# Which copy of the scores the exponential of a split-precision attention reads, and when the residual input is loaded

## The reference

```python
q_hk = (hidden_q @ Wq.T).reshape(Bv, Sv, H, K)
q_big = _apply_rope(jnp.einsum('bshk,hkq->bshq', q_hk, w_kc_q), sin_q, cos_q)
kv_r = _apply_rope(kv_c, sin_k[None], cos_k[None])
q_r = jnp.einsum('bshq,hqr->bhsr', q_big, W_qr)
k_r = jnp.einsum('bld,hdr->bhlr', kv_r, W_kr)
attn = jax.nn.softmax(jnp.einsum('bhsr,bhlr->bhsl', q_r, k_r), axis=-1)
ctx_c = jnp.einsum('bhsl,bld->bhsd', attn, kv_r)
ctx_lat = jnp.einsum('bhsd,hkd->bhsk', ctx_c, w_kc_kv)
return ctx_lat.transpose(0, 2, 1, 3).reshape(Bv, Sv, H * K) @ Wo.T

x = x + _L0_xattn_ref(_layernorm(x), ctx_512, ...)
x = x + _L0_attn_ref(_layernorm(x), ...)     # heads mix inside one token, no softmax
x = x + _L0_ffn_ref(_layernorm(x), ...)      # silu(gate) * up, integer weights with scales
```

## Time and profile before

| | |
|---|---|
| median of 3 runs | 1104.91 us (1104.62 to 1105.61) |
| the profiled execution | 1106.48 us, span 1104.7 us |
| PE busy | 1033.1 us, 94% of the span |
| DVE busy | 855.7 us, 77% |
| ACT busy | 799.8 us, 72% |
| POOL busy | 498.4 us, 45% |
| 256 maxima, lines 973 | 217.0 + 109.8 us |
| 256 exponentials, line 673 | 204.4 + 103.4 us |
| 256 low halves, line 962 | 322.3 us, DVE idle before them 87.8 us |
| 256 split passes, line 664 | 270.6 us, ACT idle before them 34.0 us |
| transposing DMAs | 256, 3.8 us from issue to landing in the median |

### The profile page before, as it was taken

The page is one execution under the profiler, slowest core; times in us unless marked ns, Lnnn a source line. Parts: engine busy times, 40 slices in busy tenths (PEclk is TensorE's granted clock), DMA queues, the critical chain, the costliest instruction groups (busy, mean ns, idle before and its releaser), DMA issues.

```text
span 1104.7 us, 24584 instructions
## 1 busy us (share of the span) xinstructions
PE 1033.1 (94%) x9456; PEld 718.9 (65%) x9456; DVE 855.7 (77%) x1177; ACT 799.8 (72%) x1380; POOL 498.4 (45%) x748
## 2 busy tenths in 40 slices
PE   4899998999999999999799999999999899999988
PEld 3444444666666677667577766776777654859877
DVE  3999888989898988888698898888898813454633
ACT  1233338899999999999799998999999932426532
POOL 1985363566767554545345454545455312000000
PEclk9999999999999999999899999999999999999989
DMA  8443365899999999999999899999998952032000
GB/s 342 132 146 114 109 138 111 180 193 204 198 202 207 207 193 199 190 188 195 192 196 193 201 179 195 192 197 194 201 193 192 192 190 105 1 132 89 1 20 20
DMA packets 568917, 180.15 MB, mean 163 GB/s; under 512 B 551520, under 2 KB 557664, under 8 KB 568160
## 3 DMA queue, kind: packets, MB, share of 16 engines
q1 hardware_dynamic: 567184, 173.33, 72.3%
q10 hardware_dynamic: 1616, 5.24, 1.5%
HBM read 39.07 MB, written 1.05 MB: 36 GB/s over the span
## 4 chain that ended last, share of the span: by engine, by line
PE 57%; DMA 13%; DVE 13%; ACT 10%; issue 6%; POOL 0%; SPq 0%; ACTq 0%; POOLq 0%; DVEq 0%
DMA pt_both<-p_both 13%; PE ps_o L1289 6%; PE ps_o L1290 6%; PE ps_o L1293 5%; PE ps_o L1350 5%; ACT prob L673 5%; DVE sized L973 4%; PE ps_s L1270 3%; PE ps_s L1271 3%; PE ps_s L1272 3%; DVE qcos L892 2%; DVE qrot L888 2%; ACT p_both L664 2%; PE ps_t L1270 2%; ACT oscl L690 2%
## 5 line engine op out<-in xcount | busy, mean ns | idle before, releaser
L962 DVE SCALAR_TENSOR_TENSOR p_both<-prob,p_both 128x1024 f16<-128x1024 f32 x256 | 322.3, 1259 | 87.8 <-ACT p_both L664 87.2
L664 ACT ACTIVATE p_both<-prob 128x1024 f16<-128x1024 f32 x256 | 270.6, 1057 | 34.0 <-DMA pt_both<-p_both 11.7
L1289 PE MATMUL ps_o<-kn,pt_both 128*128 128x128 f16 x2048 | 257.1, 219 | 27.9 <-DMA pt_both<-p_both 27.4
L1290 PE MATMUL ps_o<-kn,pt_both 128*128 128x128 f16 x2048 | 257.0, 219 | 0.0
L1289 PEld LDWEIGHTS ps_o<-kn,pt_both 128*128 128x128 f16 x2048 | 200.0, 98 | 71.7 <-DMA pt_both<-p_both 27.0
L973 DVE TENSOR_SCALAR_CACHE_REDUCE sized<-ps_s,against 128x1024 bf16<-128x1024 f32 x170 | 217.0, 1276 | 0.0
L1290 PEld LDWEIGHTS ps_o<-kn,pt_both 128*128 128x128 f16 x2048 | 200.7, 98 | 24.7
L673 ACT ACTIVATE prob<-ps_s,nmax,unscale 128x1024 f32<-128x1024 f32 x170 | 204.4, 1202 | 11.9 <-DVE sized L973 11.8
L538 POOL TENSOR_TENSOR osum<-oscl 128x256 f32<-128x256 f32 x64 | 47.9, 749 | 257.9 <-ACT oscl L690 257.9
L1293 PE MATMUL ps_o<-kn,pt_both 128*128 128x128 f16 x2048 | 156.6, 219 | 0.0
L1270 PE MATMUL ps_s<-kt,q_hi 128*128 128x512 f16 x340 | 129.3, 380 | 3.5 <-ACT prob L673 2.6
(11 more groups left out here) (215 smaller groups left out, 1849.8 us busy)
## 6 DMA issues: line engine op xcount, KB each, us to landing
wgu_raw<-w_gu_dram SPq DMA_DIRECT2D x11, 512.0 KB, 10.0
wq_s<-wq_t_dram SPq DMA_DIRECT2D x16, 256.0 KB, 3.8
wot_s<-wo_t_dram SPq DMA_DIRECT2D x16, 256.0 KB, 2.8
kvr<-ctx_kv_dram ACTq DMA_DIRECT2D x4, 1024.0 KB, 12.4
pt_both<-p_both SPq DMA_TRANSPOSE x256, 3.8
kvr<-w_mix_dram SPq DMA_DIRECT2D x4, 1024.0 KB, 9.2
wkcq_s<-w_kcq_dram SPq DMA_DIRECT2D x16, 192.0 KB, 2.4
wdn_raw<-w_dn_dram SPq DMA_DIRECT2D x1, 2816.0 KB, 8.9
```

The source lines that it names most:

```text
L664: nc.scalar.mul(p_hi(n), prob[:, n % 2, :], PSCALE).then_inc(hi_done, 1)
L962: nc.vector.scalar_tensor_tensor(out=p_lo(n), in0=prob[:, n % 2, :], scalar=PSCALE, in1=p_hi(n), op0=ALU.mult, op1=ALU.subtract).then_inc( ...
L1289: nc.tensor.matmul(o, pt_hi[:, k, :], kn[:, b, p, 0, keys], start=(k == 0), stop=False)
L1290: nc.tensor.matmul(o, pt_hi[:, k, :], kn[:, b, p, 1, keys], start=False, stop=False)
```

## The change

- The scaled scores that DVE's maximum pass writes are kept in f32, and the exponential reads them from `sized` in place of the slot in PSUM. Its scale is then the constant -1.0, in place of the operand `unscale`.
- `free_slot` waits for the maximum (`m_done`) in place of the exponential, and so do the first banks of the tail.
- The maximum of chunk n, which overwrites `sized` of chunk n-2, waits for the exponential of n-2 (`exp_done`).
- x is loaded from SP's queue behind the last transposing DMA, in place of ACT's queue at chunk 132.
- The small buffers of the softmax stand ahead of `prob`, `p_both` and `pt_both` in memory.

```diff
-                sized = sb(st, "sized", [P, 2, CHUNK], BF16)
+                sized = sb(st, "sized", [P, 2, CHUNK])
@@ block.sync, behind the loop over the transposes
+            sp.dma_start(xres[:, :, :], x_v).then_inc(x_again, 16)
             sp.wait_ge(pv_done, NCHUNK)
@@ block.scalar, exponents(n)
-                h = head_of(n)
-                nc.scalar.activation(prob[:, n % 2, :], flat(slot(n)), ACT.Exp, bias=nmax[:, i, c:c + 1],
-                                     scale=unscale[:, h:h + 1], accum_out=rsum[:, i, c:c + 1]).then_inc(exp_done, 1)
+                nc.scalar.activation(prob[:, n % 2, :], sized[:, n % 2, :], ACT.Exp, bias=nmax[:, i, c:c + 1],
+                                     scale=-1.0, accum_out=rsum[:, i, c:c + 1]).then_inc(exp_done, 1)
@@ block.scalar, loop over the chunks
-                if n == NCHUNK // B + NCH:
-
-                    act.wait_ge(pv_done, NCHUNK // B)
-                    act.dma_start(xres[:, :, :], x_v).then_inc(x_again, 16)
@@ block.vector, chunk_maximum(n)
                 if n >= 2:
-                    dve.wait_ge(m_done, n - 1)
+                    dve.wait_ge(exp_done, n - 1)
@@ block.tensor, free_slot(k)
                 if k >= RING:
-                    pe.wait_ge(exp_done, k - RING + 1)
+                    pe.wait_ge(m_done, k - RING + 1)
@@ block.tensor, empty(item), first banks of the tail
-                    pe.wait_ge(exp_done, NCHUNK)
+                    pe.wait_ge(m_done, NCHUNK)
```

More of the change, by code:

```diff
@@ L149, in build @@
                 q_lo = sb(st, "q_lo", [P, 2, P], F16)
-                sized = sb(st, "sized", [P, 2, CHUNK], BF16)
-                prob = sb(st, "prob", [P, 2, CHUNK])
-                p_both = sb(st, "p_both", [P, RING, 2, CHUNK], F16)
-                pt_both = sb(st, "pt_both", [P, TURNED, 2, CHUNK // P, P], F16)
+                sized = sb(st, "sized", [P, 2, CHUNK])
                 nmax = sb(st, "nmax", [P, 2, NCH])
@@ L162, in build @@
                 lrec = sb(st, "lrec", [P, 2, 1])
+                prob = sb(st, "prob", [P, 2, CHUNK])
+                p_both = sb(st, "p_both", [P, RING, 2, CHUNK], F16)
+                pt_both = sb(st, "pt_both", [P, TURNED, 2, CHUNK // P, P], F16)
                 oscl = sb(st, "oscl", [P, 2, NCH, P])
```

## The result

The changed kernel takes 1131.98 us in the median of four runs (1129.36 to 1135.17), beside 1105.26 for the kernel before. The ratio is 1.023, with a 95% interval of 1.020 to 1.026: slower by some 26 us, where 12.6 us less were forecast.

What follows compares the result with a forecast made beforehand. ACT's repeating pattern, 10.83 us a tile, was taken as the bound, not TensorE (10.54). Load -6.0, exponential -7.6, DMA waits +1 sum to -12.6 us: 1104.9 to 1092.3 us, own range 1089 to 1096 (chance 0.57).

Steps and rivals of the forecast that it cites:

- all six rivals: Alternative outcomes for the whole kernel: 1087 us (0.10), 1100 (0.13), 1100 (0.08), 1107.4 (0.05), 1149 (0.04), no change (0.03).
- the load of x: Moving it behind the last transpose removes ACT's 6.06 us wait at chunk 133: -6.0 us, cost 0 at its new place.
- the DMA waits: ACT's split pass waiting for transposes to land: ACT arrives 0.1 us earlier at 12 remaining waits, +1 us.
- the rival of 8.1 us: At attention's end, the load of x holds the last transpose by 8.1 us, giving 1100 us; chance 0.13.
- The exponential: On ACT, reading SBUF with one operand fewer: 1202 ns to about 1.15 us, 0.12 us a tile, -7.6 us in all.
- A tile of 10.71 us: ACT's repeating pattern over four chunks in the attention shortens from 10.83 to 10.71 us, still above TensorE's 10.54.
- the hidden operand: On ACT, overlapping passes hide the operand's saving while the SBUF read shows: +2.5 us, 1107.4 us; chance 0.05.
- the dearer f32 writes: On DVE, the f32 result slows the maximum by up to 0.57 us: +50 us less 6, 1149 us; chance 0.04.
- The score slots: TensorE may write scores about 1.3 us sooner, after the maximum; worth 0 since ACT never waits for scores, at most 3.9 us.
- the new wait on DVE: The maximum's wait for the exponential two chunks back holds nothing, as DVE's low half already waited for later ACT work; 0.

Runs made afterwards that it cites:

- a_aligned: Changed kernel plus 224 unused bytes ahead of `prob`, so `prob`, `p_both` and `pt_both` start at multiples of 512 bytes; 1095.61 us, ratio 0.990 to the kernel before.
- a_slots_exp: `a_aligned` with the score slots freed by the exponential again instead of the maximum; 1093.88 us, ratio 0.9878 to the kernel before.
- b_moved: Kernel before with only the small softmax buffers set ahead of `prob`, `p_both` and `pt_both`, which then start 288 bytes off; 1137.0 us, ratio 1.029.
- a_xmid: `a_aligned` with the load of x back at chunk 132 on ACT's queue; 1101.16 us, ratio 0.9941 to the kernel before.

## Why the prediction was wrong

The step that failed is one that the sum does not have. The section on the change names five edits, the last of them the order of the buffers, and the prediction prices four. It gave no cost to the move of `prob`, `p_both` and `pt_both`, and no rival to "the transposes become slower": all six rivals kept the transpose at its 3.7 us, or moved it once by the load of x. It enters the sum at the DMA waits: with 5.6 + 1 us there the prediction held that a transpose goes on landing before the split pass three chunks on, and in the changed kernel ACT waits 50.8 us. The move costs 1131.98 against 1095.61, or by the ratios 1.023 - 0.990 = 3.3%, some 36 us. The other terms held:

- The load of x: -6.0 forecast, -5.4 measured. At the end it disturbs nothing: in `a_aligned` the last two transposes land 4.2 and 3.8 us after their issue (4.2 and 3.7 in the kernel before, which has no load there), so the rival of 8.1 us falls, and DVE's first residual addition waits for TensorE and not for x. SP, then DVE of `a_aligned`, to be held against the earlier trace rows:

```profile
848.65 25.70 SPq L399 DMA_TRANSPOSE pt_both<-p_both  x10
874.40 0.57 SPq L417 DMA_DIRECT2D xres<-x_dram  x1
878.03 1.86 SPq L421 DMA_DIRECT2D kvr<-w_mix_dram  x4
```

```profile
893.96 0.69 DVE L987 TENSOR_TENSOR xres<-ps_o,xres 128x512 f32<-128x512 f32 x1 [21.43 <-PE ps_o L1347]
```

- The exponential: 1149 to 1155 ns forecast, 1148 measured. A tile of 10.71 us was forecast; in `a_aligned` it is 732.85 - 722.12 = 10.73:

```profile
722.12 1.16 ACT L674 ACTIVATE prob<-sized,nmax 128x1024 f32<-128x1024 f32 x1
...
727.02 1.15 ACT L674 ACTIVATE prob<-sized,nmax 128x1024 f32<-128x1024 f32 x1 [0.21 <-DVE sized L970]
...
732.85 1.16 ACT L674 ACTIVATE prob<-sized,nmax 128x1024 f32<-128x1024 f32 x1
```

The third exponential starts 4.90 us after the first, as worked out, and its wait for DVE has grown from 0.16 to 0.21 us. Both slower rivals, the hidden operand and the dearer f32 writes, fall with it.

- The score slots and the new wait on DVE: 0 forecast, nothing measurable found.
- The DMA waits: ACT's were to be 5.6 + 1 us without the load; `a_aligned` has 6.1 us in 15 times. In the changed kernel they are 50.8, in 68 times.

With the rings aligned the change gives what the sum said, -12.6 us, within the intervals: `a_aligned` has 0.9903 (-10.7 us, interval -6.5 to -14.9, on 1106.13) and `a_slots_exp` 0.9878 (-13.5 us). `a_aligned` is the changed kernel with a pad. The five kernels that have both the load at the end and the new exponential, with the source at a multiple of 256 bytes, lie at 0.988 to 0.991, with intervals that overlap.

Why 1 us of landing costs tens of microseconds of attention and not 256: the 22.6 us above are what is left after the gains. In `a_aligned` the same stretch takes 861.65 - 171.31 = 690.3 us, by its exponentials of chunks 0 and 252, so that the slower landings cost 34 us of attention:

```profile
171.31 1.15 ACT L674 ACTIVATE prob<-sized,nmax 128x1024 f32<-128x1024 f32 x1 [2.85 <-DVE sized L970]
...
861.65 1.16 ACT L674 ACTIVATE prob<-sized,nmax 128x1024 f32<-128x1024 f32 x1
```

ACT's split pass of chunk n needs the landing of n-3, and has some slack: in `a_aligned` that landing comes 1.7 us ahead of the split pass in the median, in the changed kernel 0.6. What used to be rare now holds ACT: 36 of the 256 transposes take over 5 us in `a_aligned`, 116 in the changed kernel, and 60 of its 68 waits follow one of these. The longer issue does its part. SP is more often still issuing one transpose when the low half of the next is written: 96 issues in the changed kernel began over 0.3 us after it, 87 of them right behind the issue before, and it is 91 us in sum; in `a_aligned` it is 20 issues and 15 us. The bound has moved from ACT's own work to the path through the transposes. Whether a ring of more than three places would take the price away, or the queue's own rate would hold it, no run shows.

The changed kernel (1.023) is only 0.006 under `b_moved` (1.029), about what the load's place gives alone. So the shorter exponential seems to be hidden while the rings are off; the two ran on their own, and no kernel separates them there.

Why single transposes take 5 to 6 us even when aligned, no run tests, but the traces point at something. The page of the profile has a queue that loads instructions, here in `a_aligned`:

```profile
q8 instruction: 75, 1.23, 0.5%
```

Its packets are of 16 KB, and 60 of the 75 fall into the attention. Of the 36 transposes over 5 us in `a_aligned`, 35 overlap one of these packets; of the 147 transposes that overlap none, a single one took over 5 us. In the changed kernel 101 of the 116 overlap one. That these packets are the cause is not shown by an experiment.

## What to carry to other kernels

Where a change adds or reorders buffers, compute the start of each tile that a DMA reads in small packets, before and after, and count a move as an edit with a price of its own, even if nothing reads the moved buffers differently. Small buffers set ahead of a large one cost here more than all that the change gained; a pad brings it back. And a sum whose terms are all right says nothing about an edit that has no term in it.

## What the runs showed of the hardware

- A transposing DMA within SBUF (128 partitions, 4 KB each) lands in 3.8 to 3.9 us in the median when its source starts at a multiple of 256 bytes, and in 4.8 to 4.9 when it starts 32 or 128 bytes past one; its issue on SP goes from about 1650 to about 2320 ns. The destination's start makes no difference (3.8 us at 288 past a multiple of 512).
- Of its packets of 256 bytes, 0.5% took over 25 ns with the source at a multiple of 256 bytes (`a_aligned`) and 11% with it 288 past a multiple of 512 (`after`), between 600 and 800 us; most took 18 ns in both.
- Aligned transposes of over 5 us (36 of 256 in `a_aligned`) fall, but for one, beside a 16 KB packet of the queue that loads instructions.
- With a 1 MB load issued from ACT's queue between two transposes, one transpose landed only after 11.8 us, in both kernels that had it there with the rings aligned (`before`, `a_xmid`); issued behind the last transpose in the same queue, it leaves that one at 3.8 us (`a_aligned`), beside 3.7 in the kernel before, which has no load there.
- A ScalarE pass over 1024 columns of f32 with row sums takes 1202 ns from PSUM with two per-partition operands and 1148 from SBUF with one.
